# Selective SSM mixer and expert layer on one NeuronCore: z and output projections as three split products, second convolution tap on ScalarE and POOL, a new order of the mixer step, weight split in quarters

## The reference

```python
h = _layernorm(x, axis=-1) * (1 + ca) + sa
x = x + ga * _L0_attn_ref(h, ...)          # the mixer
h = _layernorm(x, axis=-1) * (1 + cb) + sb
x = x + gb * _L0_ffn_ref(h, ...)           # 64 experts, 8 per token, and one shared
```

```python
xn = x * jax.lax.rsqrt(jnp.mean(x * x, -1, keepdims=True) + EPS) * norm_w
zxbcdt = jnp.einsum('bld,ed->ble', xn, in_proj_w)       # z 1024 | x 1024, B 128, C 128 | dt 16
conv = sum((pad[:, k:k + l, :] * conv_w[:, k] for k in range(DC))) + conv_b    # 4 taps
xBC = conv * jax.nn.sigmoid(conv)
dt = jax.nn.softplus(dt + dt_bias)
y = _ssd(xh * dt[..., None], dt * A, Bm, Cm)            # state scan in chunks of 128
y = y + D[None, None, :, None] * xh
y = y * (z * jax.nn.sigmoid(z))
y = y * jax.lax.rsqrt(jnp.mean(y * y, -1, keepdims=True) + EPS) * gnorm_w
return x + jnp.einsum('bld,ed->ble', y, out_proj_w)
```

## Time and profile before

| what | value |
|---|---|
| median of 3 runs | 5862.05 us |
| the profiled execution, span | 5864.0 us |
| the profiled execution beside the median | 2 us above it |
| busy share: PE, PEld, DVE, ACT, POOL | 96%, 73%, 61%, 45%, 60% |
| setup, until the mixer's first load | 0 to 64.75 us |
| tables, first instruction | 2728.91 us |

### The profile page before, as it was taken

One profiled execution on the slowest core, in us unless ns is written; L12 is line 12 of the kernel. 1 busy time (PEld: TensorE's weight loads), 2 busy tenths in 40 slices (PEclk: granted clock), 3 DMA queues, 4 the chain that ended last, 5 costly groups with the idle time before them and its releaser, 6 DMA issues. The chain is left out here.

```text
span 5864.0 us, 109800 instructions
## 1 busy us (share of the span) xinstructions
...
## 2 busy tenths in 40 slices
...
GB/s 209 155 149 145 165 158 143 161 148 149 169 144 155 153 143 162 149 142 137 148 215 222 196 187 224 180 160 237 154 171 197 160 161 223 212 194 180 130 274 254
DMA packets 340192, 1028.38 MB, mean 175 GB/s; under 512 B 57108, under 2 KB 61460, under 8 KB 339172
## 3 DMA queue, kind: packets, MB, share of 16 engines
...
## 5 line engine op out<-in xcount | busy, mean ns | idle before, releaser
L1339 POOL DMA_INDIRECT acc_dram<-y_e,ids x576 | 910.7, 1581 | 1111.3 <-ACT y_e L1412 687.4
L1220 PE MATMUL bank<-w_hi,x_hi 128*128 (+1 forms) x2560 | 1057.0, 413 | 0.0
L1220 PE MATMUL bank<-w_hi,x_lo 128*128 (+1 forms) x2560 | 1002.1, 391 | 0.0
L1220 PE MATMUL bank<-w_lo,x_hi 128*128 (+1 forms) x2560 | 1001.4, 391 | 0.0
L1430 DVE TENSOR_TENSOR h_lo<-bank,h_hi 128x256 fp32r<-128x256 f32 x576 | 243.7, 423 | 756.9 <-ACT h_hi L1401 756.4
L1412 ACT ACTIVATE y_e<-bank,xg_e 128x512 f32<-128x512 f32 x576 | 396.4, 688 | 691.9 <-PE bank L1220 691.9
L617 POOL DMA_INDIRECT list_dram<-tok_id,pos x512 | 595.5, 1163 | 155.9 <-issue 154.7
L1331 POOL DMA_INDIRECT xg_e<-h_dram,ids x576 | 571.2, 992 | 195.3 <-issue 174.5
L1406 ACT ACTIVATE th_f<-bank 128x256 f32<-128x256 f32 x576 | 221.3, 384 | 1015.8 <-PE bank L1220 1015.8
L783 PEld LDWEIGHTS bank<-xn_t,w_in 128*128 128x128 f32 x5120 | 587.5, 190 | 67.1 <-ACT btok L659 65.5
L783 PE MATMUL bank<-xn_t,w_in 128*128 128x131 f32 x5120 | 605.1, 276 | 14.9 <-ACT btok L659 14.2
...
## 6 DMA issues: line engine op xcount, KB each, us to landing
hi_dram<-w_hi_m SPq DMA_DIRECT2D x130, 768.0 KB, 3.3
lo_dram<-w_raw SPq DMA_DIRECT2D x130, 768.0 KB, 4.8
w_hi<-hi_dram SPq DMA_DIRECT2D x130, 768.0 KB, 7.5
w_lo<-lo_dram SPq DMA_DIRECT2D x130, 768.0 KB, 10.3
w_raw<-in_w_experts_dram SPq DMA_DIRECT2D x128, 768.0 KB, 5.0
acc_dram<-zeros SPq DMA_DIRECT2D x130, 256.0 KB, 2.8
acc_c<-acc_dram SPq DMA_DIRECT2D x128, 256.0 KB, 3.5
...
```

Of the source, the lines that this page charges most:

```text
L1220: last = nc.tensor.matmul(acc, a, b, start=(i == 0), stop=(i == len(terms) - 1))
L1339: pool.indirect_dma_start(acc_dram[r % NACC], bass.IndirectOffsetOnAxis(ap=ids[:, r:r + 1], axis=0), y[:, r % YSLOTS, :], None, compute_op ...
```

## The change

The products. `z` and the output projection are no longer eight 128x512 products of f32 each, but 24 products of fp32r each: hi*hi, hi*lo and lo*hi. Their weights are split once in the setup (`wz_hi`, `wz_lo`, `wo_hi`, `wo_lo`); the moving parts are split in every step: ScalarE makes `xn_hi` and `y_hi`, VectorE `xn_lo` and `y_lo`. For y the products with y_hi run first, and those with y_lo behind other work.

The conv. ScalarE makes tap 0 into `acc` and tap 1 into a second buffer `acc2`; VectorE adds taps 2 and 3 to `acc`; POOL adds `acc2` to `acc` before ScalarE's tanh. `y` shares its memory with `acc2`. `xbc` and `gz` have one buffer instead of two. C*B times the mask goes to a tile `cbm` in SBUF.

The weight split. A set goes in four quarters of 128x768 through two slots; quarters 0 and 2 share one, 1 and 3 the other. `split_load(sp, ws, 4)` is quarter 0 of the next set.

The order. Much of a step is rewritten: the transposes of xr, the 131-column projections, the small products and one half of the row sums now stand at the end of TensorE's step, for chunks one ahead; x1 stands one step later, at the head of VectorE's; the modulation rows are loaded in three tiles. The function of a step has arguments d to r, of which e, f, c, t and q are the same chunks as before. The zeroing of acc_dram reads a 128x128 tile four times.

The diff, cut to its core:

```diff
-PARTS, WP = 2, WPE // 2
+PARTS, WSLOT, WP = 4, 2, WPE // 4
...
-    mod = sb("mod", [P, 2, 5, DM])
-    w_in = sb("w_in", [P, KD, DIN])
-    w_out = sb("w_out", [P, KI, DM])
+    mod_a = sb("mod_a", [P, 2, DM])
+    mod_b = sb("mod_b", [P, 2, DM])
+    mod_g = sb("mod_g", [P, 2, DM])
+    w_in = sb("w_in", [P, KD, XBC + NH])
+    wz_hi = sb("wz_hi", [P, KD, DI], FP32R)
+    wz_lo = sb("wz_lo", [P, KD, DI], FP32R)
+    wo_hi = sb("wo_hi", [P, KI, DM], FP32R)
+    wo_lo = sb("wo_lo", [P, KI, DM], FP32R)
     conv_w = sb("conv_w", [P, NE, TAPS])
...
-    xbc = sb("xbc", [P, 2, NE, P])
-    gz = sb("gz", [P, 2, DI])
+    xbc = sb("xbc", [P, NE, P])
+    gz = sb("gz", [P, DI])
...
+    acc2 = sb("acc2", [P, NE, P])
+    y = acc2[:].rearrange("p n t -> p (n t)")[:, 0:DI]
...
-    if ws is not None:
-        for dram in acc_dram:
-            sp.dma_start(rows_of(dram, ws), zeros[:, 0:DM]).then_inc(s_zero, 16)
-        split_load(sp, ws, 1)
-        split_store(sp, ws, 0)
-        if not (isinstance(ws, int) and ws == NSET - 1):
-            split_load(sp, ws + 1, 0)
-    if e is not None and not (isinstance(e, int) and (e == 0 or e >= NCH - 1)):
-        sp.wait_ge(S["xg_done"], e)
-        sp.dma_start(xin[:, 1 - p, :], rows_of(x, e + 1)).then_inc(x_in[1 - p], 16)
-    if t is not None:
-        sp.wait_ge(S["h2_done"], t + 1)
-        sp.wait_ge(S["wd_done"], t + 1)
-        sp.dma_start(rows_of(h2_dram, t), h2[:, 1 - p, :]).then_inc(h2_st[1 - p], 16)
-    if ws is not None:
-        split_store(sp, ws, 1)
-    if c is not None:
-        sp.wait_ge(S["x1_done"], c + 1)
-        sp.dma_start(rows_of(x1_dram, c), x1[:, p, :]).then_inc(x1_st[p], 16)
+    if ws is not None:
+        for dram in acc_dram:
+            sp.dma_start(rows_of(dram, ws).rearrange("p (a n) -> p a n", n=P), zeros[:].unsqueeze(1).to_broadcast([P, DM // P, P])).then_inc(s_zero, 16)
+        split_load(sp, ws, 1)
+        split_store(sp, ws, 0)
+        split_load(sp, ws, 2)
+    if d is not None and d >= 2:
+        sp.wait_ge(S["xg_done"], d - 1)
+        sp.dma_start(xin[:, 1 - p, :], rows_of(x, d)).then_inc(x_in[1 - p], 16)
+    if ws is not None:
+        split_store(sp, ws, 1)
+        split_load(sp, ws, 3)
+    if t is not None:
+        sp.wait_ge(S["h2_done"], t + 1)
+        sp.wait_ge(S["wd_done"], t + 1)
+        sp.dma_start(rows_of(h2_dram, t), h2[:, 1 - p, :]).then_inc(h2_st[1 - p], 16)
+    if ws is not None:
+        split_store(sp, ws, 2)
+        split_load(sp, ws, 4)
+    if t is not None:
+        sp.wait_ge(S["x1_done"], t + 1)
+        sp.dma_start(rows_of(x1_dram, t), x1[:, 1 - p, :]).then_inc(x1_st[1 - p], 16)
+    if ws is not None:
+        split_store(sp, ws, 3)
...
+        nc.gpsimd.tensor_tensor(heads(tmp_s[:]), heads(state[:]), per_head(etk[:]), ALU.mult).then_inc(S["tmps_done"], 1)
+    if f is not None:
+        pool.wait_ge(S["taps"], XGROUPS * (f + 1))
+        nc.gpsimd.tensor_tensor(acc[:], acc[:], acc2[:], ALU.add).then_inc(S["csum_done"], 1)
+    if c is not None:
+        pool.wait_ge(S["x1s_done"], c + 1)
...
+        split_hi(act, ws, 0)
+    if c is not None:
+        act.wait_ge(S["dt_done"], c + 1)
+        at_least(act, S["ydiag_ps"], c)
+        for hh in range(NH // 2):
+            last = nc.scalar.activation(lm[:, hh * P:(hh + 1) * P], tri[:], ACT.Copy, scale=dta[:, hh:hh + 1])
+        last.then_inc(S["l_in"], 1)
+        act.wait_ge(S["xtok_ps"], c + 1)
+        at_least(act, S["x1s_done"], c)
+        at_least(act, S["yx_done"], c)
+        nc.scalar.copy(xt[:], bank[1][:]).then_inc(S["xt_sb"], 1)
+        act.wait_ge(S["small_sb"], c + 1)
+        at_least(act, S["states_ps"], c)
+        nc.scalar.activation(btok[:], half(4)[:, P:2 * P], ACT.Copy, scale=col(ends, c)).then_inc(S["btok_sb"], 1)
+    if f is not None:
+        act.wait_ge(S["xnT_ps"], f + 1)
...
+        nc.scalar.copy(xn_hi[:], xn_t[:, :, OLD:]).then_inc(S["xn_hi"], 1)
...
+        for i in group(0):
+            nc.scalar.activation(acc2[:, i, :], raw_of(i)[:, 1:1 + P], ACT.Copy, scale=conv_w[:, i, 1:2])
+            last = nc.scalar.activation(acc[:, i, :], raw_of(i)[:, 0:P], ACT.Identity, bias=conv_b[:, i:i + 1], scale=conv_w[:, i, 0:1])
+        last.then_inc(S["tap0"], 1)
...
+        act.wait_ge(S["csum_done"], f + 1)
+        at_least(act, S["yoff_ps"], f)
+        at_least(act, S["small_ps"], f)
+        at_least(act, S["xtok_ps"], f)
+        nc.scalar.activation(xbc[:], acc[:], ACT.Tanh).then_inc(S["conv_th"], 1)
...
-                last = nc.tensor.matmul(half(j), xn_t[:, k, OLD:], w_in[:, k, j * 512:(j + 1) * 512],
-                                        start=(k == 0), stop=(k == KD - 1))
+        split_products(nc, half(0), [lambda k, t=t: t[:, k, :] for t in (xn_hi, xn_lo)],
+                       [lambda k, t=t: t[:, k, 0:512] for t in (wz_hi, wz_lo)], KD).then_inc(S["z_ps"], 1)
...
-            last = nc.tensor.matmul(half(7), y_t[:, i, :], w_out[:, i, :], start=(i == 0), stop=(i == KI - 1))
+        first = [(y_hi, k, w) for k in range(KI) for w in (wo_hi, wo_lo)]
+        for i, (a, k, w) in enumerate(first):
+            nc.tensor.matmul(half(7), a[:, k, :], w[:, k, :], start=(i == 0), stop=False)
...
+            last = nc.tensor.matmul(half(7), y_lo[:, k, :], wo_hi[:, k, :], start=False, stop=(k == KI - 1))
...
+        tt(xn_lo[:], xn_t[:, :, OLD:], xn_hi[:].bitcast(FP32), ALU.subtract).then_inc(S["xn_lo"], 1)
...
-            tt(heads(lm[:, j * DI:(j + 1) * DI], 8, P), heads(lm[:, j * DI:(j + 1) * DI], 8, P),
-               half(4)[:, 0:P].unsqueeze(1).to_broadcast([P, 8, P]), ALU.mult).then_inc(S["m_done"], 1)
+        tt(heads(lm[:, 0:DI], 8, P), heads(lm[:, 0:DI], 8, P),
+           cbm[:].unsqueeze(1).to_broadcast([P, 8, P]), ALU.mult).then_inc(S["m_done"], 1)
...
-            for k in range(1, TAPS):
+        for k in range(K1, TAPS):
...
+        tt(y_lo[:].rearrange("p k t -> p (k t)"), bank[2][:], y_hi[:].rearrange("p k t -> p (k t)").bitcast(FP32), ALU.subtract).then_inc(S["ylo_done"], 1)
...
+        tt(cbm[:], half(4)[:, 0:P], tri[:], ALU.mult).then_inc(S["cb_done"], 1)
```

More of the change, by code:

```diff
@@ L792, in step @@
+                        pe.wait_ge(S["xt_sb"], c + 1)
+                        pe.wait_ge(S["l_in"], 2 * c + 2)
+                        for i in range(2):
+                            at = DI + i * 512
+                            last = nc.tensor.matmul(half(2 + i), above[:], lm[:, at:at + 512], start=True, stop=True)
+                        last.then_inc(S["rows_ps"], 1)
                     if t is not None:
                         pe.wait_ge(S["h2T_sb"], t + 1)
[L794 to L795 removed]
+                        if t + 1 < NCH:
+                            pe.wait_ge(S["btok_sb"], t + 2)
@@ new lines, in step @@
+                    if c is not None:
+                        if c + 1 < NCH:
+                            pe.wait_ge(S["taps"], XGROUPS * (c + 2))
+                            pe.wait_ge(S["dt_raw"], c + 2)
+                        else:
+                            pe.wait_ge(S["l_exp"], 2 * c + 1)
+                            at_least(pe, S["x1_done"], c)
+                        at_least(pe, S["state_done"], c)
+                        for j in range(2):
+                            last = nc.tensor.matmul(bank[3][:, j * 512:(j + 1) * 512], xbc[:, 9, :],
+                                                    state[:, j * 512:(j + 1) * 512], start=True, stop=True)
+                        last.then_inc(S["yoff_ps"], 1)
@@ new lines, in step @@
+                    if f is not None:
+                        pe.wait_ge(S["l_in"], 2 * f + 1)
+                        at_least(pe, S["rank_done"], f - 1)
+                        at_least(pe, S["yoff_sb"], f)
+                        at_least(pe, S["yT_sb"], f)
+                        at_least(pe, S["ylo_done"], f)
+                        for i in range(2):
+                            last = nc.tensor.matmul(half(6 - i), above[:], lm[:, i * 512:(i + 1) * 512], start=True, stop=True)
+                        last.then_inc(S["rows_ps"], 1)
```

666 lines of the change are left out of this document (367 added, 299 removed).

## The result

The change makes the kernel slower: 6859.56 us median of 4 runs (6854.37 to 6863.99) against 5862.06 of the kernel before, a ratio of 1.170 (95% interval 1.168 to 1.171), or 997.5 us more. The forecast was 6720 in a range of 6150 to 6900. The profiled execution has a span of 6852.6 us, 988.6 more than before.

What follows compares the result with a forecast made beforehand. TensorE was taken to set the 40.2 us step, VectorE close behind. VectorE's 34.9 + 9.6 + 1.05 + 5.9 + 3.4 = 54.9, taken as 54.0, over 62 steps added 856 to 5862: 6720 us, range 6150 to 6900.

Steps and rivals of the forecast that it cites:

- The late quarter: Quarter 0's load waits in SyncE's queue behind the h2 store, delaying ScalarE's cast and xt; VectorE waits 9.6 us a step.
- at etk: VectorE waits 1.05 us more a step for ScalarE's exps, which follow its late cast of quarter 0.
- rival two: Quarter 0 comes in time but collisions of VectorE and POOL remain: step 45.1 us, 6170 us; chance 0.10.
- The transfers: On SyncE's queue, a 384 KB quarter's store lands in 3.4 us and its load in 3.9.
- Collisions: POOL instructions hold up VectorE's with two SBUF inputs: 5.9 us a step at the router's chain, 3.4 elsewhere.
- swb would take near 3 us: Sign in VectorE's timeline: swb (L1103) near 3 us; 0.2 beside a running tap sum would mean no collision.
- the chain has a dozen short instructions with two SBUF inputs: VectorE's router chain, 4.4 us before the change, holds a dozen such instructions, now meeting POOL's work.
- VectorE's own work: VectorE's work a step without waits or hold-ups falls from 35.4 to 34.9 us.
- The 0.23 for a split product: On TensorE a split product costs 0.23 us, so 24 replace eight fp32 products: 7.03 to 5.5 us.
- costs queue time only: Zeroing in pieces of 512 B rather than 2 KB costs only queue time.
- One: Quarter 0 is late but short VectorE instructions are not held up: step 46.1 us, 6230 us; chance 0.20.
- Rival three: TensorE's saving stands and nothing replaces it: step 36.7 us, 5645 us, faster; chance 0.08.

Runs made afterwards that it cites:

- e1: The changed kernel with quarter 2's store and the next set's quarter 0 load ahead of the h2 store; 6588.8 us, step 51.93.
- e6: e1 plus tap 1 back on VectorE without POOL's sum, and a new order of the quarters' loads, stores and casts; 6185.5 us, step 45.76.
- e9: e6 plus xt*D early on POOL, and quarter 1 cast and subtracted later; 6063.3 us, ratio 1.034 to the kernel before.
- e12: The kernel before with only tap 1 moved to ScalarE and its sum to POOL; 6116.2 us, ratio 1.043.
- e5: The changed kernel with z and the output projection in plain fp32 products again; 6837.6 us, ratio 1.166.
- e4: The changed kernel with the zeroing in pieces of 1 KB instead of 512 B; 6847.8 us, step 55.99.

## Why the prediction was right, and where it was off

- **The late quarter.** Forecast 9.6, and 1.05 at etk. Measured 6.50 + 2.28 = 8.8 and 1.26. Not in the sum were quarter 2, late as well (1.16), and the acs wait (1.4), which the forecast named only in rival two. Together the waits are 12.6 for 10.65. The edits that gave the quarters room (e1 4.05, e6 4.28, e9 1.14) bring 9.5 a step. The mechanism was thus right, but "the quarter stands behind the h2 store" was less than half of it. A slot for every second quarter makes four round trips of store and load a step, and each needs room.
- **The transfers.** I took 3.4 and 3.9; the chain shows 3.80 and 3.68, and the sum of both is within 0.2. The loads of 768 KB landed in 5.0 and those of 384 KB in 3.6: 1.4 for 384 KB, so 2.2 that do not depend on size. The Trainium skill, SBUF — State Buffer, section on the DMA setup cost, has about 2 us of that kind; the trace agrees with it there, while the bytes cost 1.4 where my estimate by that page had 0.9.
- **Collisions.** Forecast 5.9 in the router and 3.4 elsewhere, measured 6.0 and 2.4. The tap sum takes 2.94 in e12, forecast 3.1. I had said that swb would take near 3 us; it takes 1.85, and sc 2.88. The step that failed is "the chain has a dozen short instructions with two SBUF inputs": the one with a single SBUF input and an SBUF output was held up as well. The Trainium skill, VectorE: DVE Perf Modes, section "What auto-detection actually checks", puts an instruction whose single source and destination lie in SBUF into the mode 2×_2P, and SBUF — State Buffer, section "SBUF: two separate sides", counts an instruction in a 2-port mode among those that need the lock. I had cited only the half on two inputs. In most steps of e12 sc is through as the tap sum begins, takes 0.18, and swb pays; in the others sc takes up to 2.96: which of the two is first decides. That the total came out close (9.3 forecast, 8.35 measured) is partly luck: xn_lo, with 1.75 the largest of the items elsewhere, was not held up at all (0.69), and a quarter subtraction that was not in the sum was (0.62).
- **VectorE's own work** was 34.9 forecast, 35.1 left over in the sum of the trace.
- **TensorE** at 73% busy in the mixer (forecast below 75%), z's second half at the lower clock (below). The granted clock fell from 0.99 to 0.86 and I had added nothing for it. In the change that is small, since e5 shows that longer products fall into the wait for the quarters; part of the acs wait may still come from it, which no run shows. e12 shows 1.4 us where TensorE's path counts. The 0.23 for a split product, which the forecast took as holding throughout, holds at the upper level only; that half of z has 0.43.
- **Zeroing** "costs queue time only": e4 agrees, as far as 1 KB against 512 B can show it.
- **The sum.** 54.9 came out and I took 54.0 for overlaps that did not occur; 56.1 was measured. The 1.2 between sum and measurement are 2.0 more of waits and 0.2 of own work, less 0.95 of collisions. Of the 140 us by which the forecast was low, 2.1 x 62 = 130 are the step, the rest the number of steps.
- **The rivals.** One (no collisions) and two (quarter in time) are both refuted: e1 to e9 show that both costs exist side by side. Rival three needed both to be absent. With the quarters in order and the tap sum gone, e9 is at 44.05: still above 40.2, since VectorE has 37.5 of own work instead of 35.4, 4.4 of collisions instead of 2.1, and 2.3 of waits. No run beat the kernel before. The single buffers of xbc and gz and the new order of TensorE's step were taken back in no run; whatever they cost is in what e9 has left. What a version with less of VectorE's work in the chain from y_done to acs would bring was not tried.
